# Experts' gating by pairs of items with identity products between them, and the first moments taken in the attention before, in a 12-layer decoder kernel on one NeuronCore

## The reference

```python
h = layernorm(x, ln1_scale, ln1_shift)
x = x + attention(h, wq, wk, wv, wo, bo)          # causal
h = layernorm(x, ln2_scale, ln2_shift)
x = x + moe_ff(h, gate_w, w1, w2, w3)
...
scores = xf @ gate_w                              # moe_ff: 256 x 8
topk_scores, topk_idx = jax.lax.top_k(scores, TOPK)   # 2 of 8
topk_probs = jax.nn.softmax(topk_scores, axis=-1)
h = jax.nn.silu(jnp.einsum('td,edh->eth', xf, w1)) * jnp.einsum('td,edh->eth', xf, w2)
out_e = jnp.einsum('eth,ehd->etd', h, w3)
```

## Time and profile before

| | us |
|---|---|
| median of 3 runs | 3028.52 |
| lowest, highest | 3020.81, 3030.66 |
| profiled execution, its own time | 3030.29 |
| its span in the trace | 3028.5 |
| PE busy in the span | 2695.7 (89%) |
| DVE, ACT, POOL busy | 1683.4, 1412.7, 1433.2 |
| chain that ended last: PE, DVE, POOL, issue, ACT | 61%, 6%, 5%, 4%, 4% |
| causal attention's last work on VectorE | 1314.4 into the span |
| first mixture: gating, routing, expert loop | 1314 to 1339, 1339 to 1358, from 1361 |
| second mixture: gating, routing, expert loop | 2300 to 2320, 2320 to 2333, from 2339.5 |

### The profile page before, as it was taken

How to read it: one execution, slowest core, us unless ns; L and a number is a source line. 1 busy time by engine, 2 the same in 40 slices (tenths; PEclk the granted TensorE clock), 3 DMA queues, 4 the chain that set the end, 5 groups by cost and what they waited for, 6 DMA issues and landing times.

```text
span 3028.5 us, 73196 instructions
## 1 busy us (share of the span) xinstructions
PE 2695.7 (89%) x26189; PEld 2213.3 (73%) x26189; DVE 1683.4 (56%) x3627; ACT 1412.7 (47%) x4543; POOL 1433.2 (47%) x1645
## 2 busy tenths in 40 slices
PE   7898898569989989969986889999996996999999
PEld 6777777436766657659985767787875995768888
DVE  6999999654456655564446753333333224555633
ACT  4666656434466657742227852323232335763310
POOL 3777777633367665543335652323322334663320
PEclk9999999779999989969997989999995998999999
DMA  3000000100000000141121020000007111011100
GB/s 100 3 2 2 2 2 2 56 30 1 24 16 14 17 20 1 56 143 48 47 68 47 0 96 12 7 10 10 7 28 247 35 35 52 0 49 32 51 10 20
DMA packets 75152, 106.25 MB, mean 35 GB/s; under 512 B 11024, under 2 KB 54672, under 8 KB 74656
## 3 DMA queue, kind: packets, MB, share of 16 engines
q1 hardware_dynamic: 68960, 86.68, 8.6%
q0 software_dynamic: 5952, 16.26, 1.7%
HBM read 88.50 MB, written 14.42 MB: 34 GB/s over the span
## 4 chain that ended last, share of the span: by engine, by line
PE 61%; DVE 6%; POOL 5%; issue 4%; ACT 4%; SPq 1%; DMA 1%; DVEq 0%; ACTq 0%; POOLq 0%
PE e_out_ps L2523 5%; PE up_ps L2503 4%; PE t_ps L674 4%; PE turn_ps L2503 4%; PE s_ps L660 3%; PE bank_a L1570 3%; PE bank_b L1570 3%; POOL probs L577 2%; PE bank_d L711 2%; ACT probs L808 2%; PE bank_a L622 2%; PE frame_ps L1649 2%; PE bank_b L1586 2%; PE bank_d L630 2%; PE bank_a L1586 2%
## 5 line engine op out<-in xcount | busy, mean ns | idle before, releaser
L577 POOL TENSOR_TENSOR probs<-probs,inv 128x512 f32<-128x512 f32 x320 | 328.0, 1039 | 266.7 <-DVE inv L933 266.4
L3464 POOL TENSOR_TENSOR hc<-h,bc 128x1024 f32<-128x1024 f32 x128 | 301.9, 2359 | 112.8 <-DVE h L3745 86.7
L808 ACT ACTIVATE probs<-s_ps,negmax 128x128 f32<-128x128 f32 (+1 forms) x768 | 297.1, 414 | 7.5 <-DVE negmax L893 6.0
L3745 DVE TENSOR_TENSOR_SCAN h<-da,dbu_ps 128x1024 f32<-128x1024 f32 x128 | 292.5, 2285 | 11.3 <-DVE dbu_ps L3757 4.2
L674 PE MATMUL t_ps<-ident,probs 128*128 128x128 f32 x1280 | 209.8, 287 | 57.6 <-POOL probs L577 49.2
L674 PEld LDWEIGHTS t_ps<-ident,probs 128*128 128x128 f32 x1280 | 140.6, 142 | 124.8 <-POOL probs L577 58.4
L3692 ACT ACTIVATE da<-dta_ps 128x1016 f32<-128x1016 f32 x128 | 130.3, 1018 | 149.1 <-PE dta_ps L3554 148.8
L3554 PE MATMUL dta_ps<-dt,a_spread 32*128 32x128 f32 x2048 | 152.6, 288 | 44.0 <-ACT da L3692 20.8
L893 DVE TENSOR_REDUCE negmax<-s_ps 128x4 f32<-128x1024 f32 (+1 forms) x128 | 156.6, 1223 | 46.2 <-PE s_ps L660 44.1
L2428 POOL DMA_INDIRECT rows<-expert_rows_in,row_from x62 | 80.8, 1303 | 208.6 <-PE x_ps L2496 192.4
L3554 PEld LDWEIGHTS dta_ps<-dt,a_spread 32*128 32x128 f32 x2048 | 128.2, 191 | 67.6 <-ACT da L3692 30.5
(11 more groups left out here) (510 smaller groups left out, 6866.2 us busy)
## 6 DMA issues: line engine op xcount, KB each, us to landing
cT<-in_ctx_turned SPq DMA_DIRECT2D x32, 256.0 KB, 2.6
w_down<-in_L_ffn_w SPq DMA_DIRECT2D x8, 1024.0 KB, 11.7
w_up<-in_L_ffn_w SPq DMA_DIRECT2D x8, 1024.0 KB, 13.4
c_in<-in_ctx SPq DMA_DIRECT2D x16, 256.0 KB, 2.7
w_gate<-in_L_ffn_w SPq DMA_DIRECT2D x8, 512.0 KB, 6.9
w_up<-in_L_ffn_w SPq DMA_DIRECT2D x8, 512.0 KB, 8.7
w_down<-in_L_ffn_w SPq DMA_DIRECT2D x8, 512.0 KB, 8.9
w_gate<-expert_rows_out SPq DMA_DIRECT2D x8, 512.0 KB, 6.5
```

The lines of the kernel that those rows point to most:

```text
L577: pool.tensor_tensor(probs[:, u % 2, i], probs[:, u % 2, i], inv[:, u % 2, HB * i:HB * (i + 1)].unsqueeze(2).broadcast_to([P, HB, W]), ALU ...
L808: last = act.activation(probs[:, u % 2, i, k, :], src, ACT.Exp, bias=negmax[:, u % 2, at], accum_out=sums[:, u % 2, at])
L3464: pool.tensor_tensor(hc[:, s % 4], h[:, s % 2], bc[:, j, 1, :].unsqueeze(1).broadcast_to([P, 2 * G, P]), ALU.mult).then_inc(hc_ready.sem, 1)
L3745: dve.tensor_tensor_scan(flat(h[:, s % 2]), flat(da[:, s % 4]), dbu_ps[s % 2][:, :, :, :].rearrange("p i g t -> p (i g t)"), 0.0, ALU.mult ...
```

## The change

There are two parts.

The gating goes by pairs of items. `turn_pair(k)` turns both items of a pair into one bank of turn_ps (four transposes), ACT copies the pair into hT, which is free until the expert loop (two passes of 128x256 with a norm, one of 128x512 without), and `gate_pair(k)` makes both items' gate products. After each pair but the last, `stream` issues three products of the identity matrix by itself, into a bank of up_ps that nobody reads. The semaphores count pairs in place of items.

The moments of items 0 to 3 and 4 to 7 are taken by VectorE within the last item of the causal attention: the first four at the begin of its last part, the others just ahead of the last residual sum. `stage.followed` tells the attention stage which stage's moments to take. Behind it VectorE normalises items 0 to 7, takes the moments of 8 to 15 and normalises them.

```diff
+def stream(pe, core, bank, count):
+
+    for _ in range(count):
+        last = pe.matmul(bank, core.ident[:, :], core.ident[:, :], start=True, stop=True)
+    return last
...
                 if not left:
                     if stage.next is not None:
                         stage.next.open_moments(dve)
+                    if stage.followed is not None:
+                        stage.followed.moments(dve, 0)
                     take_context(b, j, 0)
                     copy_probs(b, NP - 1)
...
                     take_context(b, j, 1)
+                    if stage.followed is not None:
+                        stage.followed.moments(dve, 1)
                     finish(b, j)
...
-            def turn(b):
+            def turn_pair(k):
                 ready = h_ready if pre else after.saved
-                pe.wait_ge(ready.sem, ready.done(b))
-                pe.wait_ge(xT_ready.sem, xT_ready.done(b - 2))
-                for cc in range(DC):
-                    last = pe.transpose(turn_ps[:, b % 2, cc, :], (h_all if pre else src)[:, b, cc * P:(cc + 1) * P],
-                                        core.ident[:, :])
+                pe.wait_ge(ready.sem, ready.done(2 * k + 1))
+                pe.wait_ge(xT_ready.sem, xT_ready.done(k - 2))
+                for j in range(2):
+                    for cc in range(DC):
+                        last = pe.transpose(turn_ps[:, k % 2, 2 * cc + j, :],
+                                            (h_all if pre else src)[:, 2 * k + j, cc * P:(cc + 1) * P], core.ident[:, :])
                 last.then_inc(xT_turned.sem, 1)
...
+            def gate_pair(k):
+                pe.wait_ge(xT_ready.sem, xT_ready.done(k))
+                for b in (2 * k, 2 * k + 1):
+                    for cc in range(DC):
+                        last = pe.matmul(gate_banks[b // GROUP][:, b % GROUP, :], hT[:, k % 2, 2 * cc + b % 2, :],
+                                         gw[:, cc, :], start=(cc == 0), stop=(cc == DC - 1))
                 last.then_inc(g_made.sem, 1)
+                if k < PAIRS - 1:
+                    stream(pe, core, up_ps[:, 1, 0, :], 3)
...
-            for b in range(B + 1):
-                if b < B:
-                    turn(b)
-                if b >= 1:
-                    gate(b - 1)
+            turn_pair(0)
+            for k in range(PAIRS):
+                if k + 1 < PAIRS:
+                    turn_pair(k + 1)
+                gate_pair(k)
...
+                    last = act.activation(hT[:, k % 2, 2 * cc:2 * cc + 2, :], turn_ps[:, k % 2, 2 * cc:2 * cc + 2, :],
+                                          ACT.Identity, bias=nh[:, cc:cc + 1], scale=ns[:, cc:cc + 1])
...
+                    last = act.activation(hT[:, k % 2, 0:2 * DC, :], turn_ps[:, k % 2], ACT.Copy)
...
             if pre:
-                for n in range(GROUPS + 1):
-                    if n < GROUPS:
-                        moments(n)
-                    if n >= 1:
-                        normalise(n - 1)
+                normalise(0)
+                normalise(1)
+                moments(dve, 2)
+                moments(dve, 3)
+                normalise(2)
+                normalise(3)
             for n in range(GROUPS):
                 these = slice(GROUP * n, GROUP * (n + 1))
-                dve.wait_ge(g_made.sem, g_made.done(GROUP * n + GROUP - 1))
+                dve.wait_ge(g_made.sem, g_made.done(2 * n + 1))
...
+            first_causal.followed = experts_a
```

More of the change, by code:

```diff
@@ L133, in __init__ @@
         self.start, self.next = None, None
+        self.moments, self.followed = None, None
     def leads_to(self, stage):
@@ L2262, in sparse_expert_stage @@
     GROUPS = B // GROUP
+    PAIRS = B // 2
     with ExitStack() as ctx:
@@ L2426, in fetch @@
             def fetch(i):
-                pool.wait_ge(xT_turned.sem, xT_turned.done(B + i - 2))
+                pool.wait_ge(xT_turned.sem, xT_turned.done(PAIRS + i - 2))
                 pool.indirect_dma_start(rows[:, i % 2, :], None, rows_in[0:TOKENS, :],
@@ L2474, in tensor @@
             pe.wait_ge(after.taken.sem, after.taken.done(B - 1))
-            def turn(b):
+            def turn_pair(k):
                 ready = h_ready if pre else after.saved
-                pe.wait_ge(ready.sem, ready.done(b))
-                pe.wait_ge(xT_ready.sem, xT_ready.done(b - 2))
-                for cc in range(DC):
-                    last = pe.transpose(turn_ps[:, b % 2, cc, :], (h_all if pre else src)[:, b, cc * P:(cc + 1) * P],
-                                        core.ident[:, :])
-                last.then_inc(xT_turned.sem, 1)
[L2485 to L2489, removed]
+                pe.wait_ge(ready.sem, ready.done(2 * k + 1))
[4 more added lines that the diff above has]
+                                            (h_all if pre else src)[:, 2 * k + j, cc * P:(cc + 1) * P], core.ident[:, :])
+                last.then_inc(xT_turned.sem, 1)
+            def gate_pair(k):
[4 more added lines that the diff above has]
+                                         gw[:, cc, :], start=(cc == 0), stop=(cc == DC - 1))
                 last.then_inc(g_made.sem, 1)
+                if k < PAIRS - 1:
+                    stream(pe, core, up_ps[:, 1, 0, :], 3)
             def turn_rows(i):
                 pe.wait_ge(landed[i % 2].sem, landed[i % 2].base + 16 * (i // 2 + 1))
-                pe.wait_ge(xT_ready.sem, xT_ready.done(B + i - 1))
+                pe.wait_ge(xT_ready.sem, xT_ready.done(PAIRS + i - 1))
                 for cc in range(DC):
@@ L2507, in raise_up @@
             def raise_up(i):
-                pe.wait_ge(xT_ready.sem, xT_ready.done(B + i))
+                pe.wait_ge(xT_ready.sem, xT_ready.done(PAIRS + i))
                 pe.wait_ge(w_ready.sem, w_ready.done(i))
@@ L2557, in scalar, with copy_turned @@
         def scalar(act):
-            def copy_turned(b):
-                act.wait_ge(xT_turned.sem, xT_turned.done(b))
-                act.wait_ge(g_made.sem, g_made.freed(b))
+            def copy_turned(k):
+                act.wait_ge(xT_turned.sem, xT_turned.done(k))
+                act.wait_ge(g_made.sem, g_made.freed(k))
                 for cc in range(DC if pre else 0):
-                    last = act.activation(xT[:, b % 2, cc, :], turn_ps[:, b % 2, cc, :], ACT.Identity,
-                                          bias=nh[:, cc:cc + 1], scale=ns[:, cc:cc + 1])
+                    last = act.activation(hT[:, k % 2, 2 * cc:2 * cc + 2, :], turn_ps[:, k % 2, 2 * cc:2 * cc + 2, :],
+                                          ACT.Identity, bias=nh[:, cc:cc + 1], scale=ns[:, cc:cc + 1])
                 if not pre:
-                    last = act.activation(xT[:, b % 2], turn_ps[:, b % 2, 0:DC, :], ACT.Copy)
+                    last = act.activation(hT[:, k % 2, 0:2 * DC, :], turn_ps[:, k % 2], ACT.Copy)
                 last.then_inc(xT_ready.sem, 1)
             def copy_rows(i):
-                act.wait_ge(xT_turned.sem, xT_turned.done(B + i))
+                act.wait_ge(xT_turned.sem, xT_turned.done(PAIRS + i))
                 act.wait_ge(upped.sem, upped.done(HALVES * (i - 2) + HALVES - 1))
@@ L2592, in scalar @@
             act.wait_ge(gate_loads.sem, gate_loaded)
-            for b in range(B):
-                copy_turned(b)
+            for k in range(PAIRS):
+                copy_turned(k)
             act.wait_ge(step.sem, step.done(0))
@@ L2632, in scalar, with moments @@
                     stage.next.take_second(act)
-        def vector(dve):
[L2635 to L2641, removed]
+        def moments(dve, n):
+            dve.wait_ge(after.saved.sem, after.saved.done(GROUP * n + GROUP - 1))
+            for b in range(GROUP * n, GROUP * (n + 1)):
+                dve.bn_stats(h_stats[:, b, :], src[:, b, :]).then_inc(h_stats_done.sem, 1)
+            for b in range(GROUP * n, GROUP * (n + 1)):
+                dve.wait_ge(h_stats_done.sem, h_stats_done.done(b))
+                dve.bn_aggr(h_mv[:, b, :], h_stats[:, b, :]).then_inc(h_moments.sem, 1)
+        def vector(dve):
             def normalise(n):
@@ L2836, in sparse_expert_stage @@
         for n in (xT_turned, xT_ready):
-            n.advance(B + N)
-        for n in (g_made, y_stats, y_mv, x_saved, mixed_done) + ((h_stats_done, h_moments, h_ready) if pre else ()) + (
+            n.advance(PAIRS + N)
+        g_made.advance(PAIRS)
+        for n in (y_stats, y_mv, x_saved, mixed_done) + ((h_stats_done, h_moments, h_ready) if pre else ()) + (
                 (first_scaled, part_ready) if top == 2 else ()):
@@ L2859, in sparse_expert_stage @@
         stage = Stage(sync, gpsimd, tensor, scalar, vector, done, x_saved, room=(done.sem, done.done(B - 1)))
+        stage.moments = moments
         return stage
```

## The result

| us | before | after |
|---|---|---|
| median of 5 runs | 3027.97 | 3039.71 |
| lowest, highest | 3020.81, 3030.66 | 3037.36, 3042.24 |
| profiled execution | 3030.29 | 3041.59 |

The ratio is 1.0041 with an interval of 1.003 to 1.0052: slower by 0.3 to 0.5%. Forecast were 3039.5 us in a range of 3024 to 3045.

The account below looks back on a forecast made before the run. TensorE's gating bounds the first stage; in the second a w_down load hides 3.4 us. At half clock +5.4 and +5.6 sum to +11.0 us, from median 3028.5 to 3039.5 us, range 3024 to 3045.

Parts of the forecast that it names:

- Half clock in both loops: Gate loops of both expert stages: TensorE's granted clock stays 0.50 despite the identity products, 3.7 us a pair.
- the idle time ahead: Before each gate loop: TensorE's idling, some 2 us in the first stage and 2.33 in the second, drops the clock.
- the neighbours of the loop in the earlier trace: Profile stretches compared with the loop's nine full-width passes: ten did not raise the clock, 16 back to back did.
- The products: Identity products in each gate loop: 42 passes per stage, 9.1 us at half clock, 4.8 us at full clock.
- the pair: Gate loop, two items with their identity products: 3.65 us at half clock, taken as 3.7.
- The early moments: VectorE statistics moved into the causal attention's last item: first turn 2.3 us earlier, last residual sum 0.4 us later.
- First stage: First experts' gating, from first turn to last scores seen: ends at 1344.4 against 1339.0, +5.4 us, all on the path.
- Second stage: Second experts' gating: ends 8.7 us later, partly hidden by the w_down wait; +5.6 us, bounds +3 to +8.
- the 3.4 us to spare: Second stage: rows ready at 2336.1, before the w_down load releases TensorE's turn at 2339.55; only longer delays cost.
- a second fetch that lands last: Second stage, after the delayed gating: the second fetch of rows then lands last, adding 0.3 us.
- the clock at full in both loops: Rival 1, both gate loops: products hold clock 1.00; first stage 6.3 us early, second gains nothing; 3022 us, 13%.
- Rival 3: Causal attention's end: early moments delay the last residual sum, first turn only 1.5 us earlier, half clock; 3041 us, 5%.

## Why the prediction was right

**Half clock in both loops** was its hinge, and it held. The reasons given were the idle time ahead, which the early moments only shorten, and the neighbours of the loop in the earlier trace rows. Both are borne out. The idle time was 1.61 us and the clock fell behind it; the stretch from 1330.20 had 17 matmuls at 0.50 and stayed; with six products a pair the clock rose after one stretch. The filled idle time shows the other half: at full clock the same loop holds. The fall came a little later than forecast, at 1316.5, inside the first gate products and not ahead of the loop.

The Trainium skill ("TensorE: Matmul & The Clock Gate", "Why this matters for your kernels") warns of idle gaps between bursts of products. The gaps in the change, 1.61 and 2.33 us, are shorter than those it warns of; filling them kept the clock at 1.00 all the same. Its rule that continuous work leads to the full clock is not borne out by the loop of the change, which was busy for 3.40 of 3.40 us and for 3.30 of 3.30 us in the two stretches shown and stayed at 0.50 to its end.

**The products** were priced at 42 × 0.217 = 9.1 us a stage and cost 7 × 1.48 = 10.4 less 7 × 0.10 that the next turns lost, 9.7. The difference is the first pass behind the gate products: 0.35 us to the next start in place of 0.21; no run shows why. So the pair was 3.84 us, not 3.7, and this term was mis-sized by 0.8 us in six pairs.

**The early moments**: first turn 2.3 us sooner forecast, 2.57 measured; residual sum 0.4 us later forecast, 0.3 measured. Not in the forecast was that turns which come sooner begin at the full clock: with moments alone this goes with another 0.9 us from the first turn to the last scores (1.61 + 19.31 before, 1.35 + 18.65).

**First stage**: +5.4 forecast, +5.6 measured. The dearer pair (0.8 us more) was nearly cancelled by a first turn 0.3 us earlier and a first gate product 0.2 us sooner behind it (1.79 us against 2.0).

**Second stage**: +5.6 forecast, +6.6 measured. The gating ended 9.3 us later, not 8.7 (the pair again), and the fetch took 4.07 us to its turn, not the first mixture's 3.28. This term was mis-sized: the 3.4 us to spare were only 2.6. In the trace the longer fetch is POOL's issue, 1.98 us beside VectorE's copy of weights. The 0.3 us for a second fetch that lands last did not come (2.10 us to the loop, 2.15 before). That products in the first gating only gave back 6.7 us confirms the size.

**Rivals**: the clock at full in both loops did not occur in the change, but its mechanism is real and its place was right. Its loop was put at 14.9 us from the first gate, and with the idle time filled it took 14.66. It priced the gain of the first mixture at 6.3 us; with the idle time filled the first stretch is 7.4 us shorter than before the change, and the kernel 0.35% faster (0.23 to 0.47%). Rival 3 is worth 3040.3 us by its own terms (3039.5 + 0.8), not 3041.

**The number.** That 3039.71 us were measured against 3039.5 forecast is partly luck. The stretches grew by 12.2 us, not 11.0, the median before came out at 3027.97, not 3028.5, and the rest of the profiled execution was about 1 us quicker. The mechanism and the sizes of the two stretches are what held.

## What to carry to other kernels

Work that is added to keep TensorE's clock up belongs into the idle time ahead of a thin loop (one of many short products), where here it cost nothing, and only as much into the loop as holds the clock from there. Products in a loop that already runs at half clock cost twice as much (1.48 us in place of 0.77 for three) and may not bring the clock back. Before a loop is made shorter, look for what its end waits for next: here a weight load hid one of the two loops entirely, and a long sum on another engine ate two of three us in the other. Take a change with several parts apart: of this one, a part (the moments) shortened its stretch by 3.9 us, and its loss came from one line.

## What was not expected of the hardware

One VectorE operation with two operands in the on-chip memory ended only with a long POOL sum that it began behind: 2.19 and 1.71 us in two kernels in place of 0.27, and 0.27 again when the sum was moved. Copies, maxima and index searches beside the same sum kept their times (0.19, 0.37 and 0.16 us). The Trainium skill ("SBUF — State Buffer", "SBUF: two separate sides") says that such an operation and a POOL operation take one pair of ports exclusively, and that the later one blocks; the traces agree.

A POOL fetch issued beside VectorE's copy of weights took 1.98 us to issue in place of 1.15. The Trainium skill (same page and section) has VectorE's copies keep POOL from writing its transfers' descriptions; the row agrees in sign, and no run here takes the copy away.

An identity product is two passes. Behind gate products a pass took 0.247 us on average at half clock (1.48/6) and 0.128 at full clock (0.77/6).
